# Expert down products of an attention and mixture-of-experts kernel, written as three fp32r matmuls in place of one fp32 matmul

## What is computed

```python
x = x + _L0_xattn_ref(_layernorm(x, axis=-1), ctx_1024, ctx_1024, mask, Wq, Wk, Wv, Wo, W1, b1, W2, b2, gamma, beta)
x = x + _L0_ffn_ref(_layernorm(x, axis=-1), router_w, bias, gate_w, up_w, down_w, sh_gate_w, sh_up_w, sh_down_w)

def _L0_ffn_ref(x, ...):                      # E = 16 experts, F = 128, top 4 of them in 2 of 4 groups
    topk_idx, tw = _route(x, router_w, bias)
    combine = (jax.nn.one_hot(topk_idx, E) * tw[..., None]).sum(1)
    h = jnp.einsum('td,edf->etf', x, gate_w)
    u = jnp.einsum('td,edf->etf', x, up_w)
    y = jnp.einsum('etf,efd->etd', jax.nn.silu(h) * u, down_w)
    routed = jnp.einsum('etd,te->td', y, combine)
    sh = jax.nn.silu(x @ sh_gate_w) * (x @ sh_up_w) @ sh_down_w
    return routed + sh
```

## Time and profile before

| | us |
|---|---|
| median of three runs | 341.67 (341.66 to 342.0) |
| the profiled execution | 341.1 |
| its span, first to last instruction | 339.4 |
| granted TensorE clock, mean | 0.993 of full speed |

### The profile page before, as it was taken

The page is one execution under the profiler, slowest core; times in us unless marked ns, Lnnn a source line. Parts: engine busy times, 40 slices in busy tenths (PEclk is TensorE's granted clock), DMA queues, the critical chain, the costliest instruction groups (busy, mean ns, idle before and its releaser), DMA issues.

```text
span 339.4 us, 5140 instructions
## 1 busy us (share of the span) xinstructions
PE 314.8 (93%) x1611; PEld 240.6 (71%) x1611; DVE 220.9 (65%) x568; ACT 145.5 (43%) x266; POOL 92.0 (27%) x105
## 2 busy tenths in 40 slices
PE   3989899999999998986977999999999999999993
PEld 3979789788978896874655666666666666666662
DVE  2818526948895789798676835566566656565654
ACT  2664673477347734662325342333333233333320
POOL 3006413634473444453263042000000000000000
PEclk9999999999999999999997999999999999999999
DMA  8996000000000000002100046333233333323004
GB/s 243 349 272 214 3 0 3 0 0 2 1 3 0 2 0 2 0 4 74 57 0 1 2 138 240 124 116 106 95 118 124 124 124 124 122 114 102 32 0 124
DMA packets 18773, 26.79 MB, mean 79 GB/s; under 512 B 1330, under 2 KB 13124, under 8 KB 18628
## 3 DMA queue, kind: packets, MB, share of 16 engines
q1 hardware_dynamic: 16676, 25.52, 22.8%
q10 hardware_dynamic: 2080, 1.05, 1.1%
HBM read 25.38 MB, written 1.18 MB: 78 GB/s over the span
## 4 chain that ended last, share of the span: by engine, by line
PE 76%; DVE 12%; ACT 4%; issue 3%; POOL 2%; DMA 1%; DVEq 0%; POOLq 0%; ACTq 0%
PE bank L1331 17%; PE bank L1059 12%; PE bank L1061 12%; PE bank L1060 12%; PE bank L1144 8%; PE bank L1122 7%; DVE cen L725 3%; PE bank L1171 2%; DVE sc_m L768 2%; ACT prob_T L525 2%; PE bank L1201 1%; DMA wqk_in<-in_L_xattn_Wq 1%; ACT v_o L510 1%; DVE stat L709 1%; ACT hid L535 1%
## 5 line engine op out<-in xcount | busy, mean ns | idle before, releaser
L646 ACT ACTIVATE wT<-bank 128x512 f32<-128x512 f32 x72 | 43.0, 597 | 84.9 <-PE bank L1061 84.8
L1059 PE MATMUL bank<-mT_hi,we_hi 128*128 128x512 f32 x128 | 74.0, 578 | 3.9 <-DVE wT L992 2.0
L992 DVE TENSOR_TENSOR wT<-bank,wT 128x512 f32<-128x512 f32 x64 | 44.1, 691 | 39.5 <-PE bank L1061 29.8
L1061 PE MATMUL bank<-mT_hi,we_lo 128*128 128x512 f32 x128 | 50.5, 394 | 0.0
L1060 PE MATMUL bank<-mT_lo,we_hi 128*128 128x512 f32 x128 | 50.3, 393 | 0.0
L1059 PEld LDWEIGHTS bank<-mT_hi,we_hi 128*128 128x128 f32 x128 | 24.0, 188 | 22.0 <-issue 12.3
L398 POOL TENSOR_TENSOR we_lo<-w_exp,we_hi 128x256 fp32r<-128x256 f32 x16 | 11.8, 740 | 97.8 <-ACT we_hi L567 97.8
L1331 PE MATMUL bank<-wT,we_dn 128*128 128x512 f32 x72 | 37.5, 605 | 0.0
L1331 PE MATMUL bank<-q_T,we_dn 128*128 128x512 f32 x72 | 36.5, 592 | 0.0
L1060 PEld LDWEIGHTS bank<-mT_lo,we_hi 128*128 128x128 f32 x128 | 24.1, 188 | 16.7 <-issue 14.0
L1122 PEld LDWEIGHTS bank<-cT_m,q_T 128*128 128x128 f32 x256 | 30.3, 192 | 6.4 <-DVE sc_m L768 5.9
(11 more groups left out here) (181 smaller groups left out, 529.9 us busy)
## 6 DMA issues: line engine op xcount, KB each, us to landing
wvo_in<-comb_dram SPq DMA_DIRECT2D x16, 512.0 KB, 3.5
wqk_in<-comb_dram SPq DMA_DIRECT2D x15, 512.0 KB, 3.6
mask_row<-in_mask_BxS_ff SPq DMA_DIRECT2D x1, 1024.0 KB, 8.8
out_x<-ctx_all SPq DMA_DIRECT2D x4, 256.0 KB, 2.8
x_all<-in_x SPq DMA_DIRECT2D x1, 768.0 KB, 8.2
ctx_all<-in_ctx SPq DMA_DIRECT2D x1, 768.0 KB, 10.5
wqk_in<-in_L_xattn_Wq ACTq DMA_DIRECT2D x1, 512.0 KB, 4.8
wqk_in<-in_L_xattn_Wk ACTq DMA_DIRECT2D x1, 512.0 KB, 5.6
```

The costliest lines, as they stand in the source:

```text
L646: a.activation(silu[k % 2], h_bank[k % 2][:], ACT.Silu).then_inc(silu_ready, 1)
L992: v.tensor_tensor(s_u[k % 2], u_bank[k % 2][:], silu[k % 2], ALU.mult).then_inc(s_u_ready, 1)
L1059: pe.matmul(dst, w_hi, m_hi, start=start, stop=False)
L1061: return pe.matmul(dst, w_lo, m_hi, start=False, stop=stop)
```

## The change

The down product becomes a `three` too. For that both of its operands are needed as a high and a low part.

- The down weights are rounded by ACT and their low part taken by POOL, as those of gate and up were. `we_hi` and `we_lo` are 384 columns wide, `we_dn` is gone. In the loop ACT rounds the down part of expert 2j in step k = 1 and of expert 2j + 1 in k = 5, three steps before its first use; before it copied them at k = 7 and 4.
- `act` has two buffers in place of four. ACT rounds it to `act_hi` (`act_high`), and `act - act_hi` goes to `act_lo` (`act_low`), four buffers each, in memory that the attention's folded weights had (the profile's and the order's names qk_hi, qk_lo, vo_hi, vo_lo).
- In the loop POOL does `act_low`. In the first 16 steps POOL does it for steps 0 to 3 and 8 to 11, DVE for 4 to 7 and 12 to 14. Step 15's is done in the loop.
- The wait of `weigh(n)` for `down_full` becomes one for `act_lo_ready` of step n - 2. `act_high(n)` waits for `down_full` of step n - 4, and `down(n)` waits for `act_lo_ready` of step n.
- One product in the first steps, `gate_up(0, 4)`, is moved ahead of `add_ffn(3)` on DVE.

The core of the diff:

```diff
+            def experts(j, last):                       # POOL
+                for k in range(STEPS):
+                    if k == 0:
+                        split_lo("gu", j * 2 + 1, 1)
+                    if k == 1:
+                        split_lo("dn", j * 2, 0)
+                    if k == 4 and not last:
+                        split_lo("gu", j * 2 + 2, 0)
+                    if k == 5:
+                        split_lo("dn", j * 2 + 1, 1)
+                    act_low(j, k - 1)
+
+            def act_low(j, k):                          # POOL
+                n = j * STEPS + k
+                if not (early(j) and k == 0):
+                    pool.wait_ge(act_lo_ready, n)
+                pool.wait_ge(act_hi_ready, n + 1)
+                pool.tensor_tensor(act_lo[k % 4], act[k % 2], act_hi[k % 4].bitcast(F32),
+                                   ALU.subtract).then_inc(act_lo_ready, 1)
...
+            def act_high(j, k):                         # ACT
+                n = j * STEPS + k
+                if weighted(n):
+                    a.wait_ge(weighed_ready, weighed_count(n))
+                else:
+                    a.wait_ge(s_u_ready, n + 1)
+                if not (early(j) and k < 4):
+                    a.wait_ge(down_full, n - 3)
+                a.copy(act_hi[k % 4], act[k % 2]).then_inc(act_hi_ready, 1)
...
                     gate(j, k)
-                    if k == 7 and not last:
-                        a.wait_ge(down_full, j * STEPS + CH)
-                        hold_down(j * 2 + 2, 0)
+                    act_high(j, k - 1)
...
             def weigh(j, k):                            # DVE
                 v.wait_ge(s_u_ready, n + 1)
-                v.wait_ge(down_full, n - 3)
+                v.wait_ge(act_lo_ready, n - 1)
                 v.wait_ge(weighed_ready, weighed_count(n - 1))
...
-                v.tensor_tensor(act[k % 4], s_u[k % 2], comb[i][:, c * CW:(c + 1) * CW],
+                v.tensor_tensor(act[k % 2], s_u[k % 2], comb[i][:, c * CW:(c + 1) * CW],
                                 ALU.mult).then_inc(weighed_ready, 1)
...
-                pe.matmul(acc[c][:], we_dn[i][:], act[k % 4], start=start, stop=stop).then_inc(down_full, 1)
+                pe.wait_ge(act_lo_ready, n + 1)
+                three(acc[c][:], we_hi[i][:, 2 * P:], we_lo[i][:, 2 * P:], act_hi[k % 4], act_lo[k % 4],
+                      start, stop).then_inc(down_full, 1)
```

More of the change, by code:

```diff
@@ L139, in build @@
         silu, s_u, act = ([wT_flat[:, 2 * a + i, :] for i in range(2)] for a in range(3))
[L140 to L142 removed]
+        act_hi = [w[:].rearrange("p h k -> p (h k)")[:, i * CW:(i + 1) * CW] for w in (qk_hi, qk_lo) for i in range(2)]
+        act_lo = [w[:, i * CW:(i + 1) * CW] for w in (vo_hi, vo_lo) for i in range(2)]
         comb_dram = nc.dram_tensor("comb_dram", [2, NE, T // 2], F32, kind="Internal").ap()
@@ L454, in mT_low @@
                                    ALU.subtract).then_inc(mT_lo_ready, 1)
-            split_lo(3, 3)
+            for part in ("gu", "dn"):
+                split_lo(part, 3, 3)
+            act_low(0, 0)
             inverse_root(3, CH - 2)
+            act_low(0, 1)
             add_b2(CH - 1)
+            act_low(0, 2)
+            act_low(0, 3)
             weigh(4)
@@ L466, in _ @@
             weigh(7)
+            for k in range(8, 12):
+                act_low(0, k)
             weigh(12)
             weigh(13)
-            split_lo(4, 0)
+            split_lo("gu", 4, 0)
             weigh(14)
@@ L600, in _ @@
                 if c == CH:
-                    split_hi(3, 3)
-                    hold_down(3, 3)
+                    for part in ("gu", "dn"):
+                        split_hi(part, 3, 3)
                 if last:
@@ L637, in _ @@
                         a.wait_ge(ld_exp, 6 * 16)
-                    split_hi(c - 1, c - 1)
-                    hold_down(c - 1, c - 1)
+                    for part in ("gu", "dn"):
+                        split_hi(part, c - 1, c - 1)
             def gate(j, k):
@@ L684, in _ @@
             router_sigmoid(1)
-            for k in range(9, 14):
+            act_high(0, 7)
+            for k in range(9, 13):
                 gate(0, k)
+                act_high(0, k - 1)
+            gate(0, 13)
             first_weights(CH // 2)
@@ L992, in gate_up, with act_low @@
                 v.tensor_tensor(s_u[k % 2], u_bank[k % 2][:], silu[k % 2], ALU.mult).then_inc(s_u_ready, 1)
+            def act_low(j, k):
+                n = j * STEPS + k
+                if early(j) and k - 1 in POOL_LOW:
+                    v.wait_ge(act_lo_ready, k)
+                v.wait_ge(act_hi_ready, n + 1)
+                v.tensor_tensor(act_lo[k % 4], act[k % 2], act_hi[k % 4].bitcast(F32),
+                                ALU.subtract).then_inc(act_lo_ready, 1)
             def weigh(j, k):
@@ L1015, in _ @@
             gate_up(0, 3)
+            gate_up(0, 4)
             add_ffn(CH - 1)
             statistics(2, CH - 1, z)
-            gate_up(0, 4)
             gate_up(0, 5)
+            act_low(0, 4)
             residual(CH - 1)
@@ L1024, in _ @@
             take_logits(CH - 2)
+            act_low(0, 5)
             gate_up(0, 7)
+            act_low(0, 6)
             gate_up(0, 8)
@@ L1031, in _ @@
             group_scores(1)
+            act_low(0, 7)
             gate_up(0, 9)
@@ L1038, in _ @@
             take_combine(1)
-            for k in range(12, 16):
-                gate_up(0, k)
+            gate_up(0, 12)
+            gate_up(0, 13)
+            gate_up(0, 14)
+            act_low(0, 12)
+            gate_up(0, 15)
+            act_low(0, 13)
+            act_low(0, 14)
             with v.Fori(2, NX // 2) as j:
```

100 lines of the change are left out of this document (55 added, 45 removed).

## The result

The changed kernel takes 348.67 us (median, 348.31 to 350.16), against 341.75 for the kernel before (341.66 to 342.0): a ratio of 1.021, 95% interval 1.0179 to 1.024. The profiled execution took 348.89 us, of which 346.1 are its span. So the change makes the kernel 2.1% slower; 346.0 was predicted.

What follows compares the result with a forecast made beforehand. PE was taken to bound the kernel before, and weigh and POOL excluding each other the changed loop. Loop +2.7, early part +1.2 and end +0.4 gave +4.3 us: 346.0 us, range 335 to 352.

Steps and rivals of the forecast that it cites:

- the port: SBUF access that weigh on DVE and POOL's low part share under an exclusive lock, each waiting out the other's instruction.
- the ring of two: In the loop, act's two buffers make each weighing wait for the low part of two steps back, so both run in pairs.
- the chain: Loop waits among weighing, rounding and low part set the step, not PE: 2.22 to 2.40 us, chance 0.65.
- the gain on PE: Three fp32r matmuls (0.69 us) replace one fp32 product (0.86): 9.5 us over 56 steps, if other engines keep pace.
- The loop's step: Time per loop step, taken as 2.29 us against 2.241 before: +2.7 us over 55 steps.
- no race lost: In the loop, weigh always gets ahead of POOL where they compete: 2.25 us a step; one loss in eight gives 2.34.
- w: End of a weighing in the loop; next weigh asks at +0.77 or +0.94 us, POOL at +0.83 to +0.89.
- The early part: Ahead of the loop: shorter PE idle times against POOL delaying routing and the last steps; +1.2 us, range -1.5 to +3.
- The extra splits in the attention block: nothing: Four more POOL splits of 0.47 us ahead of the loop, POOL 27% busy: no cost, at worst +0.5 us.
- The end: After the last weighing, rounding, low part and three matmuls take 3.1 us where 2.65 was: +0.4 us.
- The first rival: PE's pace holds in the loop, without mutual exclusion or growing lag: 331.0 us, chance 0.12.
- POOL wins most races: Rival: in the loop POOL asks before weigh, or the lock lasts longer; 2.5 us a step, 357.5 us, chance 0.10.

Runs made afterwards that it cites:

- e1: Changed kernel with four buffers for act in place of two, weigh waiting for the low part of four steps back: 339.19 us, ratio 0.9918.
- e2: Changed kernel with gate_up writing its loop product back into its PSUM bank and weigh reading it there, two act buffers kept: 337.88 us, ratio 0.9884.
- e6: e5 with weigh reading its product from PSUM as in e2: 334.73 us, ratio 0.9787 to the kernel before.
- e7: e6 with four buffers of act in place of two: 334.56 us, ratio 0.9797 to the kernel before.
- e5: Changed kernel with its first 16 steps taken back to those of before (fp32 down products, no rounding or low parts): 359.5 us, ratio 1.0514.
- e8: e5 with four buffers of act, weigh still reading from SBUF: 358.94 us, ratio 1.0481 to the kernel before.
- e9: Changed kernel with one more long-true DVE wait ahead of each loop weighing, needing its own register instruction: 368.41 us, ratio 1.0775.
- e12: e8 with the new counters started at 16 and 4, so loop waits compare with the changed kernel's numbers: 335.83 us, ratio 0.982.

## Why the prediction was right, and where not

- **The outcome and its mechanism.** Slower, 348.67 in a range of 335 to 352, by the port and the ring of two: right, and shown for this kernel by e1 and e2, each of which takes out one of the two and is over 9 us faster. But the share of each term is not as forecast: the chain eats up the gain on PE and adds next to nothing (0.3 us in the loop, where 2.7 of 4.3 were forecast), and the kernel is slower for what happens ahead of the loop. `weigh` has a mean of 1.07 us in the page (1.1 or more was forecast), the low parts have 1.67 and 1.49 for 1.28, and they come in pairs. By the Trainium skill, "SBUF — State Buffer", section "Who interferes with whom", a DVE instruction with at most one input in SBUF, outside its two-port modes, does not contend with GpSimd; e2's means of 692 and 1296 ns agree.
- **The loop's step.** 2.29 was taken, between no race lost (2.25) and one in eight (2.34). It is 2.246: no race is lost. The walk to 2.25 was right to 0.01. What was off were its two requests: POOL asks at w + 0.73 and not at 0.83 to 0.89, and `weigh` at w + 0.63 to 0.72 and not at 0.77. The handovers are shorter than the rows taken for them: ACT starts 0.03 after the weighing (0.08 was taken), POOL 0.07 to 0.08 after ACT (0.13 to 0.19, from a row with a register instruction in it), and DVE's gap is 0.03 to 0.12 where the changed loop has fewer register instructions than that of before. The two errors all but cancelled; the term is 0.3 us where 2.7 was in the sum. That no race is lost hangs on 0.01 us in one step of eight.
- **The early part.** +1.2 was in the sum (range -1.5 to +3), +5.6 measured: the mis-sized term, outside its own range. It was -1.5 for PE's idle times, +2.4 for routing, and so +0.3 for the last four steps. Measured were 0 up to 184.7, +3.0 for routing, and +2.7 from there to the first weighing. The gain of 1.5 us did not come: DVE's norms at the end of the attention block meet splits and low parts too, 1.1 and 2.0 us at 157.45 and 163.22. That these ate the gain is not shown; they were left out of the walk in any case. The prediction had only instructions with two inputs in SBUF in view; these have one, and are held up. The trace of before had it already: 1.12 us for four undisturbed, 1.50 beside a split. In routing low part 11 costs `comb_w` 0.9 us (197.53, 1.32 for 0.40) and not 0.4. In the last steps the first weighing itself waits (1.50 for 0.76), and an `act_low` on DVE for ACT behind POOL's last weighings (3.04 for 2.54). "The extra splits in the attention block: nothing" also looked at POOL's busy share, not at whom POOL holds up.
- **The end.** 0.9 for 0.4: POOL's last two low parts ran as a pair, since the first had waited behind the last weighing (335.26, x2, 3.01 us).
- **PE.** 9 matmuls at 0.233 are 2.10 a step, not 2.07 to 2.08. Rounding the cadence to 0.23 overrated the gain of an undisturbed loop, 9.5 us. The first rival's 331.0 holds that and 1.5 us from ahead of the loop. e6 and e7 have its undisturbed loop behind the first steps of before: 2.109 and 2.108 a step are 7.3 us in 55, and the times are 334.73 and 334.56.
- **The rivals.** "POOL wins most races" had 2.5 to 2.7 us a step and 357.5: e5, e8 and e9 are it, at 2.53 to 2.61, e8 with four buffers. Its point of decision was named right (POOL ahead of `weigh`), but the 0.10 that it got rested on two handovers that must fit in 0.15 us. They take 0.11, so POOL asks at w + 0.73, before the w + 0.77 that was to decide it. Only the shorter gap on DVE kept `weigh` ahead, by 0.01 to 0.10 us. The sum hit near the median since its errors had opposite signs, -2.4 in the loop against +4.4 and +0.5 around it, which is luck and not accuracy.

## What to carry to other kernels

When two engines keep each other out, ask first whether the delayed result is waited for within a step. One operand left in PSUM took the contention away in every run that had it (e2, e6, e7). Four buffers in place of two made it nearly free in e1 and e12 (2.0755 and 2.126 us a step), but not in e8 (2.562), where the helper engine asks first in each step. And look at the order of instructions between two dependent operations: a semaphore wait whose number needs a fresh register can decide who is first, so let the counters of a loop run in step with its index. Ahead of a loop, a helper engine's new work is to be held against every instruction on the critical path there that it can hold up, those with one input too, not against its own busy share.
